# A graph network's first stage: the first two tiles share the weights, and the edge counts start with the third tile

## The chip, the cores and the metric

The kernel runs on one core of one Trainium2 chip. The metric is the device time of one execution in microseconds (us); lower is better. Engines are called as in the profile: PE (TensorE matmul), PEld (its weight load), DVE (VectorE), ACT (ScalarE), POOL (GpSimd), SP (SyncE, which issues most DMAs). PEq, DVEq, SPq and ACTq are the sequencers of these engines.

## What is computed

The input is x (1250 nodes, 1024 features) and 40,000 edges, sorted by their destination. The first block of the reference, cut to what matters:

```python
norm_x = weight * (x * rsqrt(mean(x**2) + EPS))
out = norm_x @ W_root + bias                    # 1024 -> 286
for r in range(2):
    w = (edge_type == r)
    sums = segment_sum(norm_x[src] @ W_rel[r] * w[:, None], dst)
    cnt = segment_sum(w, dst)
    out = out + sums / maximum(cnt, 1)[:, None]
x = layernorm(x + x + elu(out) @ wo)
```

A second block follows (an encoder, three rounds of summing neighbours with a small perceptron, a decoder). The change doesn't touch it.

## The kernel before, in words

The nodes are cut into T = 10 tiles of P = 125. Stage 1 does two things side by side.

**The projections.** For each tile, PE turns x (8 blocks of 128 features, `turn(q, v)` turns four of them into PSUM bank 6 + q), ACT copies them to `xnT` with the norm's weight as scale (`weigh(q)`), and PE multiplies each block by the 858 columns of the three weight matrices in `w_all` (`products(u, v)`, L781, two matrix products of 429 columns for block u). After block 7 ACT writes the tile out (`evacuate`: `y_root`, `y_hi`, `y_f`), and POOL makes `y_lo` from it (L388).

**The edge counts.** The edges stand in G = 80 rows of 500. For each row DVE builds one-hot codes in bf16: `codes` (L1234), `lows` (L1226) and `weighed_codes` (L1239). PE multiplies them (`count(b)`, L759, four small products), and DVE adds the two halves of the result into `cnt` (`place`, L1259) at a column that it reads from `mini` with `bases` (L1251). There are two sets of buffers, so the codes of row g + 2 are built while row g is placed. ACT takes finished columns of `cnt` apart into `adj`, a part of DONE columns at a time (`part(k, cols)`).

Everything is ordered by hand: each engine runs its own list, with semaphores between them. Tile 0 goes through the weights alone, in a list of its own. Its blocks wait for five pieces of the weights (`PIECES`: blocks 0, 1, 2 and 3, 4 and 5, 6 and 7), and between its blocks PE turns the edge data into PSUM (`turn_edges`, L752; the bounds of the rows, L836). From tile 1 on, PE does a row of edges before each block and one more at block 4: UG = 9 rows a tile, and the last tile has the 8 that are left. On PE and DVE tiles 1 to 8 run in a loop of two tiles; the last tile is written out behind it. For each tile, DVE also takes one reciprocal at the sixth row (L1270).

Stage 2 (`relations`, L937 and L939) multiplies `adj` by `y_hi` and `y_lo`. PE begins it when `adj_done` is set, which DVE does behind the last placed row (L1323), when the first part of `adj` is made, and when the `y_lo` of all tiles but the last is there. SP loads `cb_b` for it when `adj_done` is set and the last product of stage 1 is done (L304).

At the start SP issues x of tile 0, the norm's weight, the five pieces of the weights, and then x of tile 1. ACT's queue issues the three lists of the edges (`dst_i`, `src_i`, `typ_i`, L504).

Of the kernel before, what the change touches and what calls it, by code (L numbers as in the profile page):

```python
# [26 lines left out]
P = 125  # L27
# [24 lines left out]
DONE = 2 * P  # L52
FAR = 1e6
ROUND = 1.5 * 2 ** 18
UG = KD + 1
# [8 lines left out]
def graph_kernel(nc, x, src, dst, typ, ln_w, w_rel, w_root, conv_b, wo, g_in, b_in, w1, b1, w2, b2,  # L64
                 wa, ba, wb, bb, ng, nb, wd1, bd1, wd2, bd2, g_out, b_out, out):
    with ExitStack() as ctx:
# [28 lines left out]
        lo_base = y_base + size([P, T, YH], F32R)  # L95
        y_f = at(lo_base, "y_f", [P, T, 2 * F], F32)
# [144 lines left out]
        tails_set = sem("tails_set")  # L241
        second_set, parted, codes_set = sem("second_set"), sem("parted"), sem("codes_set")
# [38 lines left out]
        def _(sp):  # L281
# [151 lines left out]
        def _(act):  # L433
            for s in (xnT_copied, y_copied, hT_lo, r1_done, d1_done):
                act.sem_inc(s, 1)
# [31 lines left out]
            def evacuate(t, v):  # L467

                wait_apart(act, proj_mm, 1 + t * 2 + 2)
# [11 lines left out]
            def tile_of_1(t, v, uses, last, cleared=None, complete=None):  # L481
# [14 lines left out]
                if complete is not None:  # L496
                    act.wait_ge(counts_free, complete * (2 * UG) + 2 * UG + 2)
                    part(complete, bass.ds(complete * DONE, DONE))
# [4 lines left out]
            for a, d, done in ((dst_i, dst, dst_in), (src_i, src, src_in), (typ_i, typ, typ_in)):  # L503
                act.dma_start(a[:], d.rearrange("(g e) -> g e", g=G)).then_inc(done, 16)  # L504
# [3 lines left out]
            act.wait_ge(xnT_ps, 1)  # L508
            weigh(0)
            act.wait_ge(xnT_ps, 2)  # L510
            weigh(1)
            squares(0, 0)
            root_of(0, 0)
            act.wait_ge(edges_ps, 1)
            act.copy(value[:, 0:G], pb[0:P, 4, 160:160 + J * G].rearrange("p (j g) -> p g j", j=J)).then_inc(far_copied, 1)
            act.wait_ge(codes_ready, 1)
            act.copy(farC[:, 0:G], pb[0:P, 1, 0:J * G].rearrange("p (j g) -> p g j", j=J)).then_inc(far_copied, 1)
            act.wait_ge(xnT_ps, 3)
            act.wait_ge(proj_mm, 1 + 1)
            weigh(0)  # L520
            squares(1, 1)
            root_of(1, 1)
            evacuate(0, 0)
            tile_of_1(1, 1, 64, False, C0)
            tile_of_1(2, 0, 64, False)
            with act.Fori(1, T // 2 - 2) as i:
                tile_of_1(i * 2 + 1, 1, i * 32 + 64, False, i * CS + C0)
                tile_of_1(i * 2 + 2, 0, i * 32 + 64, False, None, i - 1)
            tile_of_1(T - 3, 1, 32 * (T // 2 - 1) + 32, False)
            tile_of_1(T - 2, 0, 32 * (T // 2 - 1) + 32, False, None, T // 2 - 3)  # L530
            tile_of_1(T - 1, 1, None, True, None, T // 2 - 2)
            act.wait_ge(counts_free, G + 2)
            part(T // 2 - 1, slice(N - DONE, N))
# [212 lines left out]
        def _(pe):  # L746
# [3 lines left out]
            def turn_edges(f, a, c0=0):  # L750
                for j in range(J):
                    ins = pe.transpose(pb[0:P, f, c0 + j * G:c0 + (j + 1) * G], a[:, j * P:(j + 1) * P], ident[0:G, 0:G])  # L752
# [33 lines left out]
            def tile_of_1(t, v, g0, odd, rows, uses):  # L786

                def row(r):
                    pe.wait_ge(onehots, g0 + r + 1)
                    pe.wait_ge(counts_free, g0 + r + 1)  # L790
                    count((odd + r) % 2).then_inc(counts_mm, 1)

                extra = rows - KD
                for u in range(KD):
                    row(u if u <= 4 else u + extra)
                    if u == 0:
                        pe.wait_ge(xnT_copied, 1 + t * 2)
                        turn(1, v)
                        pe.wait_ge(xnT_copied, 1 + t * 2 + 1)
                        pe.wait_ge(y_copied, t)  # L800
                    if u == 4:
# [4 lines left out]
                        if extra:  # L806
                            row(5)
# [16 lines left out]
            warm(2, 5)  # L824
            for u in range(KD):
                if u == 0:
                    pe.wait_ge(xnT_copied, 1 + 1)
                if u == 4:
                    pe.wait_ge(xnT_copied, 1 + 2)
                for q, ks in enumerate(PIECES):  # L830
                    if u == ks[0]:
                        pe.wait_ge(w_in[q], 48)
                if u == 2:
                    pe.wait_ge(bounds_ready, 1)
                    for i in range(2 * H):
                        ins = pe.transpose(pb[0:1, 4 + i // H, i % H * G:(i % H + 1) * G], bounds[:, i:i + 1], ident[0:G, 0:G])  # L836
                    ins.then_inc(bounds_ps, 1)
                if u == 4:
                    pe.wait_ge(lows_ready, 1)
                    turn_edges(0, e_low)  # L840
                if u == 5:
                    pe.wait_ge(edges_ready, 1)
                    pe.wait_ge(prep, 9)
                    turn_edges(4, e_val, 160)
                    turn_edges(1, e_code).then_inc(edges_ps, 1)
                if u == KD - 1:
                    pe.wait_ge(xs_in[1], 32)
                    turn(0, 1)
                products(u, 0)
# [789 lines left out]
```

## Time and profile before

| what | value |
|---|---|
| median of 3 runs | 577.02 us (575.8 to 577.03) |
| the profiled execution: its own time | 575.35 us |
| its span, first to last instruction | 573.5 us |
| PE / PEld busy | 556.0 us (97%) / 399.0 us (70%) |
| DVE / ACT / POOL busy | 371.2 us (65%) / 243.3 us (42%) / 101.6 us (18%) |
| the first product of stage 1 starts | 8.82 us |
| stage 2 starts | 158.05 us |

The span leaves out 1.85 us of the execution's own time. The matrix products' ends are modelled, so PE can look busy where it is waiting; starts are the safer figure. Consecutive instructions of DVE overlap by a few tens of nanoseconds, so for DVE, too, the distance from start to start is what is counted below.

### The profile page before, as it was taken

The numbers are of one execution on the slowest core, as the hardware profiler recorded it, in microseconds if no ns is written. First come the engines' busy times: TensorE is split into PE (matmuls) and PEld (weight loads), VectorE is DVE, ScalarE is ACT, GpSimd is POOL, SyncE is SP. The second block draws the span as 40 slices with busy tenths as digits, with TensorE's granted clock in tenths as the row PEclk, the third lists the DMA queues.
The fourth block names the chain that finished last, engine by engine and source line by source line (L and its number), as shares of the span: only waits on it lengthen the run. The fifth ranks groups of instructions, "written<-read, shape, count | busy, mean of one in ns | idle before, by whom it ended". The sixth has DMA issues, their size and how long they took to land.

```text
span 573.5 us, 8850 instructions
## 1 busy us (share of the span) xinstructions
PE 556.0 (97%) x2708; PEld 399.0 (70%) x2708; DVE 371.2 (65%) x1070; ACT 243.3 (42%) x484; POOL 101.6 (18%) x80
## 2 busy tenths in 40 slices
PE   7999999999999999999999999999999999999992
PEld 3555555555598989888889888868868867555541
DVE  8588888888748898987331130048658667855555
ACT  3553464636565555652222121023232233367555
POOL 4010000000000000030544442102202220132130
PEclk9999999999999999999999999999999999999997
DMA  8511000111031312147200001500100100022123
GB/s 263 159 38 36 24 25 24 36 36 36 2 93 38 73 37 72 37 136 210 101 2 0 0 0 40 191 1 1 38 0 0 37 0 2 0 73 68 39 73 107
DMA packets 20963, 30.77 MB, mean 54 GB/s; under 512 B 5458, under 2 KB 15404, under 8 KB 20928
## 3 DMA queue, kind: packets, MB, share of 16 engines
q1 hardware_dynamic: 20512, 29.66, 17.6%
q10 hardware_dynamic: 416, 0.67, 0.4%
q8 instruction: 19, 0.31, 0.2%
q14 instruction: 16, 0.13, 0.1%
HBM read 25.20 MB, written 5.12 MB: 53 GB/s over the span
## 4 chain that ended last, share of the span: by engine, by line
PE 77%; DVE 9%; DVEq 5%; issue 5%; DMA 2%; SPq 1%; ACT 1%; POOL 0%
PE banks L989 12%; PE banks L1075 12%; PE banks L906 12%; PE banks L781 7%; PE banks L874 5%; PE banks L1011 5%; PE banks L1001 4%; PE banks L937 4%; PE banks L939 4%; DVEq L1251 3%; PE banks L916 3%; PE banks L1065 3%; DVE cnt L1259 2%; DVE oh_both L1239 2%; DVE oh_both L1234 1%
## 5 line engine op out<-in xcount | busy, mean ns | idle before, releaser
L781 PE MATMUL banks<-w_all,xnT 128*125 128x429 f32 x320 | 131.8, 535 | 1.3 <-DMA w_all<-in_L_gnn_W_rel 1.3
L781 PEld LDWEIGHTS banks<-w_all,xnT 128*125 128x125 f32 x320 | 54.0, 188 | 30.4 <-issue 28.6
L906 PE MATMUL banks<-hT,w_s 128*128 128x250 f32 x320 | 68.9, 375 | 0.1
L906 PEld LDWEIGHTS banks<-hT,w_s 128*128 128x128 f32 x320 | 60.3, 190 | 8.4 <-issue 1.4
L937 PE MATMUL banks<-y_hi,adj 125*125 125x288 f32 x200 | 55.2, 304 | 0.5 <-issue 0.5
L1259 DVE TENSOR_TENSOR cnt<-cnt,banks 125x110 f32 x160 | 42.4, 265 | 18.1 <-issue 12.6
L939 PE MATMUL banks<-y_lo,adj 125*125 125x286 f32 x200 | 53.5, 295 | 0.0
L1406 DVE TENSOR_SCALAR hT<-banks,g_c,b_c 128x125 f32<-128x125 f32 x60 | 19.4, 399 | 45.1 <-PE banks L891 45.0
L989 PE MATMUL banks<-adj,h_hi 125*128 125x250 f32 (+1 forms) x180 | 48.3, 367 | 0.2
L759 PEld LDWEIGHTS banks<-oh_both,oh_low 125*128 125x128 bf16 x320 | 23.1, 98 | 34.9 <-issue 20.1
L989 PE MATMUL banks<-adj,h_lo 125*128 125x250 f32 (+1 forms) x180 | 45.7, 353 | 0.0
L1075 PE MATMUL banks<-wd_s,dT 128*125 128x512 f32 x96 | 42.7, 592 | 0.0
L399 POOL TENSOR_TENSOR h_lo<-h,h_hi 125x256 fp32r<-125x256 f32 x30 | 21.8, 733 | 108.5 <-ACT h_hi L608 108.5
L937 PEld LDWEIGHTS banks<-y_hi,adj 125*125 125x125 f32 x200 | 37.2, 186 | 3.8 <-issue 3.8
L388 POOL TENSOR_TENSOR y_lo<-y_f,y_hi 125x572 fp32r<-125x572 f32 x10 | 12.8, 1276 | 140.6 <-ACT y_f L479 140.6
L939 PEld LDWEIGHTS banks<-y_lo,adj 125*125 125x125 f32 x200 | 37.3, 187 | 0.0
L874 PE MATMUL banks<-wo_s,yT 128*125 128x256 f32 x160 | 36.2, 379 | 0.0
L463 ACT ACTIVATE xnT<-banks,lnw 128x125 f32<-128x125 f32 x80 | 22.7, 385 | 29.4 <-PE banks L775 29.4
L1226 DVE TENSOR_TENSOR oh_low<-iota_l,edge 125x512 bf16<-125x512 f16 x80 | 34.4, 430 | 0.1
L989 PEld LDWEIGHTS banks<-adj,h_hi 125*128 125x128 f32 x180 | 29.6, 189 | 6.0 <-issue 2.1
L1234 DVE TENSOR_TENSOR oh_both<-iota_m,edge 125x440 bf16<-125x440 f16 x80 | 33.4, 418 | 0.0
L989 PEld LDWEIGHTS banks<-adj,h_lo 125*128 125x128 f32 x180 | 30.1, 189 | 4.6
(222 smaller groups left out, 943.0 us busy)
## 6 DMA issues: line engine op xcount, KB each, us to landing
xt<-in_x SPq DMA_DIRECT2D x15, 448.0 KB
out_x<-ot SPq DMA_DIRECT2D x9, 448.0 KB
w_s<-in_L_gnn_W SPq DMA_DIRECT2D x5, 512.0 KB, 6.4
xn<-in_x SPq DMA_DIRECT2D x5, 448.0 KB
wd_s<-in_L_gnn_Wd SPq DMA_DIRECT2D x1, 2048.0 KB, 13.5
w_all<-in_L_gnn_W_rel SPq DMA_DIRECT2D x6, 286.0 KB, 6.7
wo_s<-in_L_gnn_wo_weight SPq DMA_DIRECT2D x1, 1024.0 KB, 6.1
w_all<-in_L_gnn_W_root SPq DMA_DIRECT2D x3, 286.0 KB, 6.3
```

The source lines that it names most:

```text
L759: ins = pe.matmul(pb[:, b, q * C:(q + 1) * C], oh_low[:, b, q, :, j], oh_both[:, b, q, :, j], start=(j == 0), stop=(j == JH - 1))
L781: ins = pe.matmul(pb[0:P, 2 + 2 * v + n, 0:FH], xnT[:, u], w_all[:, u, n * FH:(n + 1) * FH], start=(u == 0), stop=(u == KD - 1))
L874: pe.matmul(pb[0:P, 4 + q, 512 - QW:512], yT[:, i], wo_s[:, i, q * QW:(q + 1) * QW], start=(i == 0), stop=False)
L906: ins = pe.matmul(pb[:, b0 if f == 0 else 4 + f % 2, 0:2 * P], w1_s[:, k, f * 128:(f + 1) * 128], hT[:, k], start=(k == 0), stop=(k == KD ...
L937: pe.matmul(pb[0:P, b + r, 0:F + 2], mine, y_hi[:, s, r * (F + 2):(r + 1) * (F + 2)].bitcast(kind), start=(s == 0), stop=False)
L939: ins = pe.matmul(pb[0:P, b + r, w0:w0 + F], mine, y_lo[:, s, r * F:(r + 1) * F].bitcast(kind), start=False, stop=(s == T - 1))
L989: ins = pe.matmul(pb[:, 3 * f + c, 0:n], part[:, s, f * 128:(f + 1) * 128], adj[:, 0, s, c0:c0 + n], start=(s == 0 and part is h_hi), stop ...
L1011: ins = pe.matmul(pb[0:P, 6 + t % 2, 0:HB], rT[:, k, t * P:(t + 1) * P], wb_s[:, k], start=(k == 0), stop=(k == K2 - 1))
L1075: ins = pe.matmul(pb[0:P, 2 + 2 * u + q], (dT, dT_odd)[c % 2][:, k, u * P:(u + 1) * P], wd2_s[:, k, q * 512:(q + 1) * 512], start=(k == 0) ...
L1226: return dve.tensor_tensor(oh_low[:, b], both(iota_l, LOW), spread_out(edge[:, 0], g, LOW), ALU.is_equal)
L1234: return dve.tensor_tensor(oh_both[:, b], both(iota_m, C), spread_out(edge[:, 1], g, C), ALU.is_equal)
L1259: dve.tensor_tensor(cols, cols, window(b, q), ALU.add).then_inc(done, 1)
```

## The change

The first two tiles go through the weights together: blocks 0 and 1 of tile 0, blocks 0 and 1 of tile 1, blocks 2 and 3 of tile 0, and so on. Tile 1 gets a second buffer for its turned x (`xnT1`), and its own turns stand between its blocks and those of tile 0. The edge counts begin with tile 2, and all eight tiles from there on have UG = 10 rows, all of them in the loop. Columns of `adj` are made in parts of 300 (`PARTED`). SP issues x of tile 1 behind the second piece of the weights, and the edge lists, which ACT's queue issued before, behind the third.

```diff
-DONE = 2 * P
+DONE = 300
+PARTED = (0, DONE, 2 * DONE, 3 * DONE, 1060, N)
-UG = KD + 1
+UG = KD + 2
+        xnT1 = at(lo_base + 2 * 4 * 2 * F, "xnT1", [128, KD, P], F32)
...
             load_x(0, 0)
             sp.dma_start(lnw8[:], ln_w.rearrange("(k p) -> k p", p=128)).then_inc(lnw_in, 16)
-            for q in range(len(PIECES)):
-                load_w(sp, q)
+            load_w(sp, 0)
+            load_w(sp, 1)
             load_x(1, 1)
+            load_w(sp, 2)
+            for a, d, done in ((dst_i, dst, dst_in), (src_i, src, src_in), (typ_i, typ, typ_in)):
+                sp.dma_start(a[:], d.rearrange("(g e) -> g e", g=G)).then_inc(done, 16)
+            load_w(sp, 3)
+            load_w(sp, 4)
...
+            def weigh_blocks(t, turned):
+                for k in range(KD):
+                    act.wait_ge(xnT_ps, 1 + 2 * t + k // 4)
+                    act.activation(turned[:, k], pb[:, 6 + k // 4, k % 4 * P:(k % 4 + 1) * P], ACT.Copy,
+                                   scale=lnw[:, k:k + 1]).then_inc(first_turned, 1)
+            weigh_blocks(0, xnT)
             squares(0, 0)
             root_of(0, 0)
+            weigh_blocks(1, xnT1)
+            squares(1, 1)
+            root_of(1, 1)
+            act.wait_ge(xs_in[0], 64)
+            act.wait_ge(xn_rstd, 1)
+            squares(2, 0)
+            root_of(2, 0)
...
-            evacuate(0, 0)
-            tile_of_1(1, 1, 64, False, C0)
-            tile_of_1(2, 0, 64, False)
+            evacuate(0, 0, 4)
+            evacuate(1, 1, 5)
+            tile_of_1(2, 0, 64, False, C0)
+            tile_of_1(3, 1, 96, False)
...
                 for u in range(KD):
-                    row(u if u <= 4 else u + extra)
+                    row(u + (u > 0) + (u > 4))
                     if u == 0:
                         pe.wait_ge(xnT_copied, 1 + t * 2)
                         turn(1, v)
+                        row(1)
...
-            warm(2, 5)
-            for u in range(KD):
+            warm(1, 5)
+            def first_products(u, t):
+                pe.wait_ge(first_turned, KD * t + u + 1)
+                for n in range(2):
+                    ins = pe.matmul(pb[0:P, 2 + 2 * t + n, 0:FH], (xnT, xnT1)[t][:, u], w_all[:, u, n * FH:(n + 1) * FH],
+                                    start=(u == 0), stop=(u == KD - 1))
+            for u0 in range(0, KD, 2):
+                for t in range(2):
+                    if t == 1 and u0 == 0:
+                        pe.wait_ge(xs_in[1], 32)
+                        pe.wait_ge(first_turned, KD)
+                        turn(0, 1)
+                        turn(1, 1)
+                    if t == 1 and u0 == 2:
+                        pe.wait_ge(bounds_ready, 1)
...
+                    if t == 1 and u0 == 4:
+                        pe.wait_ge(lows_ready, 1)
+                        pe.wait_ge(edges_ready, 1)
...
+                        turn_edges(0, e_low)
+                        turn_edges(7, e_val)
+                        turn_edges(1, e_code).then_inc(edges_ps, 1)
+                    if t == 0 and u0 == 6:
+                        pe.wait_ge(xs_in[0], 64)
+                        turn(0, 0)
+                    for u in (u0, u0 + 1):
+                        for q, ks in enumerate(PIECES):
+                            if u == ks[0] and t == 0:
+                                pe.wait_ge(w_in[q], 48)
+                        first_products(u, t)
...
-            with pe.Fori(0, T // 2 - 1) as i:
-                tile_of_1(i * 2 + 1, 1, i * (2 * UG), 0, UG, i * 32 + 64)
-                tile_of_1(i * 2 + 2, 0, i * (2 * UG) + UG, UG % 2, UG, i * 32 + 64)
+            with pe.Fori(0, T // 2 - 2) as i:
+                tile_of_1(i * 2 + 2, 0, i * (2 * UG), i * 32 + 64)
+                tile_of_1(i * 2 + 3, 1, i * (2 * UG) + UG, i * 32 + 96)
...
-            tile_of_1(T - 1, 1, (T - 2) * UG, 0, G - (T - 2) * UG, None)
+            tile_of_1(T - 2, 0, 6 * UG, 32 * (T // 2))
+            tile_of_1(T - 1, 1, 7 * UG, None)
...
                 with dve.Fori(0, T // 2 - 1) as i:
                     dve.wait_ge(adj_rest, i + 1)
-                    tile_of_1(i * 2 + 1, 1, i * (2 * UG), 0, UG, placed)
-                    tile_of_1(i * 2 + 2, 0, i * (2 * UG) + UG, UG % 2, UG, placed)
-                tile_of_1(T - 1, 1, (T - 2) * UG, 0, G - (T - 2) * UG, placed)
+                    tile_of_1(i * 2 + 2, 0, i * (2 * UG), placed)
+                    tile_of_1(i * 2 + 3, 1, i * (2 * UG) + UG, placed)
```

DVE now builds codes for two rows beyond the last (before, it left them out: the lines `more` and `if more:` are gone), and its test of the data (`gaps`, `signs`, `bign`: which column each row may touch, and when) has the new bounds of 300, 600, 900 and 1060 columns in place of multiples of 250.

## Rows read from the trace of the kernel before

**Rows 1.** The page: busy time of each engine over the span.

```profile
PE 556.0 (97%) x2708; PEld 399.0 (70%) x2708; DVE 371.2 (65%) x1070; ACT 243.3 (42%) x484; POOL 101.6 (18%) x80
```

**Rows 2.** Busy time in two stretches, one tile each: PE, PEld, DVE, ACT, POOL, clock.

```profile
113.50:128.76 15.26, 15.05 (x80) 8.30 (x77) 13.22 (x47) 5.54 (x16) 1.23 (x1) 1.00 0.12 34
128.76:143.57 14.81, 14.81 (x81) 8.40 (x77) 13.18 (x48) 10.02 (x18) 1.34 (x1) 1.00 0.12 35
```

**Rows 3.** Who waited for whom, 20 to 158 us: in total, times, longest.

```profile
PEld banks L759 <- DVE oh_both L1239: 13.8, 44, 1.2
```

**Rows 4.** The chain that ended last: start, length, piece.

```profile
15.63 0.40 PE banks L752 x4
17.51 0.83 PE banks L752 x8
21.27 0.43 PE banks L775 x4
21.70 1.45 PE banks L781 x4
```

**Rows 5.** PE in order of time: start, length, instruction.

```profile
120.72 0.37 PE L759 MATMUL banks<-oh_both,oh_low 125*128 125x110 bf16 x4
120.94 0.60 PE L775 MATMUL banks<-ident,xt 125*128 125x125 f32 x4
121.70 0.39 PE L759 MATMUL banks<-oh_both,oh_low 125*128 125x110 bf16 x4 [0.17 <-DVE oh_both L1239]
...
123.43 0.37 PE L759 MATMUL banks<-oh_both,oh_low 125*128 125x110 bf16 x4
```

**Rows 6.** DVE in order of time: the first row of edges, and two in the loop.

```profile
23.77 0.38 DVE L1234 TENSOR_TENSOR oh_both<-iota_m,edge 125x440 bf16<-125x440 f16 x1
...
87.24 0.37 DVE L1234 TENSOR_TENSOR oh_both<-iota_m,edge 125x440 bf16<-125x440 f16 x1
...
88.80 0.38 DVE L1234 TENSOR_TENSOR oh_both<-iota_m,edge 125x440 bf16<-125x440 f16 x1
```

**Rows 7.** DVE in order of time: behind POOL, and around the loop's ends.

```profile
71.39 0.97 DVE L1234 TENSOR_TENSOR oh_both<-iota_m,edge 125x440 bf16<-125x440 f16 x1
...
83.00 0.38 DVE L1234 TENSOR_TENSOR oh_both<-iota_m,edge 125x440 bf16<-125x440 f16 x1
...
85.13 0.38 DVE L1234 TENSOR_TENSOR oh_both<-iota_m,edge 125x440 bf16<-125x440 f16 x1
...
115.22 0.38 DVE L1234 TENSOR_TENSOR oh_both<-iota_m,edge 125x440 bf16<-125x440 f16 x1
```

**Rows 8.** POOL in order of time.

```profile
70.91 1.20 POOL L388 TENSOR_TENSOR y_lo<-y_f,y_hi 125x572 fp32r<-125x572 f32 x1 [14.64 <-ACT y_f L479]
```

**Rows 9.** The lead-in, PE and DVE in order of time.

```profile
7.76 0.66 DVE L1161 TENSOR_REDUCE fourths<-dst_i 80x4 f32<-80x500 int32 x1
...
8.82 3.12 PE L781 MATMUL banks<-w_all,xnT 128*125 128x429 f32 x8 [1.26 <-DMA w_all<-in_L_gnn_W_rel]
...
12.22 0.86 DVE L1180 SCALAR_TENSOR_TENSOR e_code<-dst_i,bounds,e_blk 80x250 f32<-80x250 int32 x2
12.27 0.44 PE L836 MATMUL banks<-ident,bounds 80*1 80x80 f32 x4 [0.32 <-DMA w_all<-in_L_gnn_W_rel]
...
22.98 0.37 PE L759 MATMUL banks<-oh_both,oh_low 125*128 125x110 bf16 x4
```

**Rows 10.** DMA rate, 0 to 60 us in 40 slices of 1.5 us.

```profile
GB/s 0 221 161 258 317 304 349 355 353 366 390 303 268 46 5 0 52 284 5 0 11 0 0 0 0 5 101 240 5 0 0 0 0 0 0 5 145 197 0 0
```

**Rows 11.** The end of stage 1, PE in order of time.

```profile
158.05 0.37 PE L937 MATMUL banks<-y_hi,adj 125*125 125x288 f32 x1 [0.47 <-issue]
...
168.22 0.43 PE L866 MATMUL banks<-ident,ybuf 125*128 125x125 f32 x2 [0.40 <-DVE tails L1355]
```

**Rows 12.** Busy time in two stretches at the span's end; columns as in Rows 2.

```profile
563.00:567.00 4.00, 0.15 (x1) 0.00 (x0) 3.41 (x10) 2.72 (x5) 0.00 (x0) 1.00 0.01 3
567.00:571.00 4.00, 0.00 (x0) 0.00 (x0) 2.25 (x9) 2.61 (x6) 0.00 (x0) 0.50 0.44 138
```

More of the change, by code:

```diff
@@ L433, in _ @@
         def _(act):
-            for s in (xnT_copied, y_copied, hT_lo, r1_done, d1_done):
+            for s in (xnT_copied, xnT_copied, xnT_copied, xnT_copied, xnT_copied, y_copied, hT_lo, r1_done, d1_done):
                 act.sem_inc(s, 1)
@@ L496, in tile_of_1 @@
                 if complete is not None:
-                    act.wait_ge(counts_free, complete * (2 * UG) + 2 * UG + 2)
-                    part(complete, bass.ds(complete * DONE, DONE))
+                    k, cols, rows = complete
+                    act.wait_ge(counts_free, rows + 2)
+                    part(k, cols)
                 evacuate(t, v)
@@ L532, in _ @@
+            tile_of_1(T - 2, 0, 32 * (T // 2), False, None, (2, slice(PARTED[2], PARTED[3]), 6 * UG))
+            tile_of_1(T - 1, 1, None, True, None, (3, slice(PARTED[3], PARTED[4]), 7 * UG))
             act.wait_ge(counts_free, G + 2)
-            part(T // 2 - 1, slice(N - DONE, N))
+            part(4, slice(PARTED[4], N))
             def elu_parts_of(t):
@@ L784, in products, with tile_of_1 @@
                     ins.then_inc(proj_mm, 1)
-            def tile_of_1(t, v, g0, odd, rows, uses):
+            def tile_of_1(t, v, g0, uses):
                 def row(r):
@@ L805, in tile_of_1 @@
                             turn(0, 1 - v)
-                        if extra:
-                            row(5)
+                        row(6)
                     products(u, v)
@@ L823, in _ @@
             turn(1, 0)
-            warm(2, 5)
-            for u in range(KD):
[L826 to L849, printed above, removed]
+            warm(1, 5)
@@ new lines, in first_products @@
+            def first_products(u, t):
[3 more added lines that the diff above has]
+                                    start=(u == 0), stop=(u == KD - 1))
+                if u in (3, KD - 1):
+                    ins.then_inc(proj_mm, 1)
+            for u0 in range(0, KD, 2):
[7 more added lines that the diff above has]
+                        pe.wait_ge(bounds_ready, 1)
+                        for i in range(2 * H):
+                            ins = pe.transpose(pb[0:1, i // H, i % H * G:(i % H + 1) * G], bounds[:, i:i + 1], ident[0:G, 0:G])
+                        ins.then_inc(bounds_ps, 1)
+                    if t == 1 and u0 == 4:
+                        pe.wait_ge(lows_ready, 1)
+                        pe.wait_ge(edges_ready, 1)
+                        pe.wait_ge(prep, 9)
+                        pe.wait_ge(first_turned, 2 * KD)
+                        turn_edges(0, e_low)
[9 more added lines that the diff above has]
+                        first_products(u, t)
@@ L925, in relations @@
                         pe.wait_ge(pre_elu, t - 1)
-                    if t % 2 == 0:
-                        pe.wait_ge(parted, t // 2 + 1)
+                    pe.wait_ge(parted, sum(c0 < (t + 1) * P for c0 in PARTED[:-1]))
                     b = 2 * (t % 2)
@@ L1261, in place, with tile_of_1 @@
                     dve.sem_inc(done, 1)
-            def tile_of_1(t, v, g0, odd, rows, placed):
+            def tile_of_1(t, v, g0, placed):
                 base = bases(g0)
-                for u in range(rows):
+                for u in range(UG):
                     if u == 5:
@@ L1274, in tile_of_1 @@
                     place(base, b, 0, placed, first_added)
-                    more = rows == UG or u + 2 < rows
-                    if more:
-                        codes(g + 2, b).then_inc(codes_set, 1)
-                        lows(g + 2, b)
+                    codes(g + 2, b).then_inc(codes_set, 1)
+                    lows(g + 2, b)
                     dve.wait_ge(first_added, g + 1)
                     place(base, b, 1, placed, counts_free)
-                    if more:
-                        weighed_codes(g + 2, b).then_inc(onehots, 1)
-                    if u + 1 < rows:
+                    weighed_codes(g + 2, b).then_inc(onehots, 1)
+                    if u + 1 < UG:
                         base = bases(g + 1)
```

49 lines of the change are left out of this document (21 added, 28 removed).

## The prediction

> **What bounds the kernel now.** I read the page first, then the stretches of stage 1, then each engine's beat in it. By the page PE is busy 97% of the span and DVE 65% [rows 1], which reads like a kernel bound by PE alone. The stretches of stage 1 say nearly the same: in two tiles PE is busy 15.05 of 15.26 us and 14.81 of 14.81 us, DVE 13.22 and 13.18 [rows 2]. But the table of waits has PE's weight loads for the edge rows waiting 44 times for DVE's one-hot codes [rows 3]. So the question for this stage is how near DVE is to being the bound, and the starts of its instructions answer that better than busy time.
>
> *PE's beat.* The two products of one block take 1.45 us, four turns 0.43 us [rows 4]. The tile from 128.76 to 143.57 us took 14.81 us with no wait [rows 2]; it has eight blocks, nine edge rows and eight turns, so an edge row costs (14.81 - 8 x 1.45 - 2 x 0.43) / 9 = 0.26 us. From 121.70 to 123.43, one edge row and one block, it is 1.73 - 1.45 = 0.28. With four turns between two rows they are 0.98 us apart, with a wait for DVE in it, against 0.26 + 0.43 = 0.69 [rows 5]. The tile ahead of the undisturbed one took 15.26: it waited 0.45 us [rows 2].
>
> *DVE's beat.* Inside the loop one row of edges takes DVE 1.56 us from code to code (87.24 to 88.80), and this beat is the same in some 50 of the 70 rows [rows 6]. It is DVE's own speed: it is faster than PE's 1.45 + 0.26 = 1.71, so between the waits DVE is catching up. The other rows are longer. One per tile is long because its code takes 0.97 us where it takes 0.38 otherwise, while POOL makes `y_lo` [rows 7, 8]. At the loop's end the distance is 85.13 - 83.00 = 2.13, that is 0.57 more [rows 7]. All in all two tiles, 18 rows, took DVE 115.22 - 85.13 = 30.09 us [rows 7]. 18 x 1.56 is 28.08, so 2.01 us are extras of the pair: twice POOL (0.55 each), once the loop's end (0.57), and 0.34 for two reciprocals and small things. PE alone needs 2 x 14.81 = 29.62 for the same pair. DVE is thus already the bound of the loop, by 0.5 us a pair, and nothing is left for a tenth row.
>
> **The change, part by part.**
>
> *The start.* Before, PE waits until 8.82 us for the first piece of the weights, 1.26 us of it as the product's last wait [rows 9]. The piece is issued as before, but ACT's queue no longer puts 0.48 MB of edges beside it. At the 258 to 317 GB/s of those slices [rows 10] 0.48 MB are some 1.6 us. The first product could so come up to 1.3 us earlier (then x's turns, and what PE runs to keep warm, end at about 7.5) or no earlier. I take the middle, 8.0 us; ends 7.5 and 8.8.
>
> *The lead-in.* From there to the first edge row PE has 16 blocks, 16 x 1.45 = 23.2; twice four turns for tile 1 and four for tile 2, 1.29; the bounds, 0.44, and the edge data, 0.40 + 0.83 [rows 4]: 26.2 us. Behind tile 1's turns PE waits for ACT's first copy, some 0.2. Sum 26.4, so the first edge row is at 8.0 + 26.4 = 34.4 us, where it was at 22.98 [rows 9]. The difference, 11.4, is the second tile's 11.6 of products and 0.4 of turns, less what the start gives back.
>
> *What the shared weights save.* Before, the only later wait for the weights ended at 12.27 and was 0.3 us on PE [rows 9]. That goes away; there was hardly a DMA stall in tile 0 to remove. New waits: x of tile 1 is now wanted at 8.0 + 2.9 = 10.9. Ahead of it are x, two pieces of weights and itself, 1.9 MB, which at the rates of [rows 10] had moved by 9.0 us. Then it needs its turn and landing, so between 0 and 1 us of wait; I take 0. The edges come behind 2.8 MB, that is at about 13.3 us instead of 7.8. DVE's work on them, 12.22 + 0.86 - 7.76 = 5.3 us [rows 9], ends at about 18.6. PE wants the bounds at 8.0 + 10.2 = 18.2, which DVE makes about 2.3 us after the first list, at 15.6, and the rest at 24.3. The cover is thin by 2.6 us at the first place and wide at the second. The codes of rows 0 and 1 are made well ahead of 34.4. The later pieces of the weights land before 18 us [rows 10] and are wanted at 21 and 27. All this costs nothing. With the two ends of the start and of these waits the first edge row is at 33.9 to 36.2.
>
> *The edge rows.* They stay 80, with the same instructions on PE (L759) and DVE (L1234, L1226, L1239, L1259), but nothing of them is done before 34.4. PE's tile of ten rows is 14.81 + 0.26 = 15.07. DVE's pair of tiles is 20 rows, 20 x 1.56 + 2.01 = 33.2 us, or 16.6 a tile: 1.5 more than PE's. So DVE sets the beat, and PE, with only two sets of codes between them, waits for it at nearly every row; it is those waits that take the place of the gain. DVE begins its first code 23.77 - 22.98 = 0.8 us after PE's first row [rows 6, 9], at 35.2. Four pairs less the last loop's end are 4 x 33.2 - 0.6 = 132.2, so DVE is done at 167.4. Ends: if POOL no longer held DVE up at all, 4 x 1.1 less; if each pair had 0.2 more, 0.8 more. I take the pair as measured, since POOL's `y_lo` follows each tile's evacuation just as now. The tile that stood behind the loop, where rows are written out, is now in the loop as well; that is in the 33.2. So are the codes of two rows beyond the last, which before were left out.
>
> *The end of the stage.* Before, PE's own products ended the stage: stage 2 starts at 158.05 [rows 11]. Now `adj_done` does, at 167.4, as DVE is about one row behind PE: PE's last product is over at about 166.3, so ACT's evacuation and POOL's last `y_lo` are early rather than late. Smaller parts of `adj` (300, 160 and 190 columns) are off the path, since stage 2 wants the first at once, when it has long been made, and the last for its ninth tile. `cb_b` is loaded when `adj_done` is set. It was issued 0.39 us ahead of stage 2 and the chain through it made PE wait 0.40 at 168.22 [rows 11]; now it is issued at the same moment, so 0 to 0.4 more. I take 0.2.
>
> **The sum.** Stage 2 at 167.4 instead of 158.05 is +9.35, `cb_b` +0.2: +9.5 us, and everything behind shifts by it. Against the profiled execution, 575.35 + 9.5 = 584.9. The median of the runs is 1.67 above that execution, so the forecast is 577.0 + 9.5 = 586.5 us.
>
> **Rivals.**
> *PE stays the bound and the change gains* (faster). For this speaks busy time: PE 15.05 against DVE 13.22 in one tile [rows 2]. Then eight tiles of 15.07 from 34.4 end at 155.0, and stage 2 starts at 155.4, 2.6 us earlier: 574.4 us. It decides if DVE does ten rows with all extras in under 15.07, 1.51 a row instead of 1.66. Against it: the row of 1.56 repeats unchanged over the loop. The Trainium skill ("Perfetto Trace Analysis", Identifying the Most-Contended Engine) takes occupancy as the fair measure for Vector, and by it DVE at 13.2 of 15 has room for one more row; the starts in this trace say that it hasn't, as a fixed 0.2 us per row is spent between instructions.
> *Half and half* (about the same). If DVE had slack that I don't see, as rows that wait for PE without the profile saying so, a row might be 1.45 and the end of the stage near 158: 577 us. The pair of 30.09 against PE's 29.62 speaks against it.
> *TensorE's clock falls* (much slower). PE will now wait for a good 1 us in each 16. If it fell from 2.4 to 1.2 GHz, a block would take 2.9 us, a tile some 27, and each tile at the low clock cost 10 us more. In this trace the granted clock stays 1.00 with such waits as there are [rows 2], and falls to 0.50 only after PE has had nothing to do for some 4 us at the end [rows 12]. The Trainium skill ("TensorE: Matmul & The Clock Gate", HAM oscillation) tells of gaps that throttle PE again and again, there while PE waits for whole transfers; no run so far shows it here, where the longest single wait is 1.2 [rows 3].
> *The test of the data fails.* Row 20 must start at column 300 or later; evenly spread edges put it at 1250 x 20 / 80 = 312. If it failed, all counts would be made again by the slow way, 114 sweeps over 80 rows, at over 1 us a row more than 9 ms. The reference's edges are spread closely enough.
>
> **Chances.** DVE-bound as summed: 0.86; its own range is 584.5 to 588.5, from the first row's place (-0.5 to +1.8), the pairs (most of -4.4 is excluded by the rows, I keep -1.5) and the 0.6 us by which runs differ. PE-bound gain: 0.05. Half and half, anywhere from 575 to 583: 0.04. Slower than 589, by a late transfer or the clock: 0.04. The test: 0.01. For 8 in 10 the range is 583.3 to 589.0. Faster by over 0.3% (what a measurement can tell, 1.7 us) 0.06, within it 0.02, slower 0.92.
>
> **What would show it.** The first product at about 8 us and the first edge row (L759) at 34 to 35. L1234 every 1.56 us and every 33.2 us per pair, to the end. The waits of L759 for L1239 up from 13.8 us to some 25 to 30 (80 rows, 1.5 us in each tile on top of now). PE's busy share in 36 to 166 us below its share now, its clock 1.00. Stage 2 at about 167.4, released by DVE's memset (L1323), and the distance from there to the end as before. The forecast is wrong if DVE's row gets shorter than 1.51 with extras, if the first row comes much later than 36, or if stage 2 and what follows change length.

## The result, and the profile after

The changed kernel takes 587.71 us (median of 4 runs, 586.64 to 588.37), the kernel before 577.02 beside it: a ratio of 1.0191, 95% interval 1.0171 to 1.0210. The forecast was 586.5 us, in a range from 583.3 to 589.0. By the medians the change costs 10.7 us, where the sum had 9.5. The profiled execution took 586.64 us with a span of 584.8, that is 11.3 us more than the one before; the traces below explain this difference of 11.3.

The page of the changed kernel, busy time of each engine; then two of its stretches, as in [rows 2], the first in the loop of the counted tiles, the second the end of the stage:

```profile
PE 558.8 (96%) x2707; PEld 398.3 (68%) x2707; DVE 373.4 (64%) x1077; ACT 243.7 (42%) x484; POOL 101.7 (17%) x80
```

```profile
96.00:126.00 30.00, 28.11 (x144) 15.25 (x142) 26.36 (x91) 16.70 (x31) 2.51 (x2) 1.00 0.12 34
...
156.00:168.00 12.00, 10.79 (x52) 5.69 (x52) 10.60 (x40) 1.64 (x2) 0.00 (x0) 1.00 0.01 1
```

PE is at 94% and 90% there, where a tile before had 99 to 100% [rows 2]. The granted clock is 1.00 there, as in all of stage 1. The engine that now sets the pace shows 26.36 of 30 us busy, 88%: DVE doesn't look full by its busy time either.

Who waited for whom, 34 to 168 us of the changed kernel, against [rows 3]:

```profile
PEld banks L776 <- DVE oh_both L1271: 32.2, 68, 2.0
...
PE banks L776 <- DVE oh_both L1271: 9.4, 16, 1.3
```

L776 is the edge row's product on PE (L759 before), L1271 the weighed codes (L1239 before). For the 80 rows there are 68 waits of the weight loads for DVE, against 44, and they add up to 32.2 us, a little above the 25 to 30 forecast.

PE in order of time: the first product, tile 1's turns, the bounds, the first edge row and the first product of stage 2, against [rows 9, 11]:

```profile
7.48 3.15 PE L846 MATMUL banks<-w_all,xnT 128*125 128x429 f32 x8
...
11.01 1.08 PE L792 MATMUL banks<-ident,xn 125*128 125x125 f32 x8 [0.39 <-DMA xn<-in_x]
...
18.00 0.44 PE L861 MATMUL banks<-ident,bounds 80*1 80x80 f32 x4
...
34.49 0.37 PE L776 MATMUL banks<-oh_both,oh_low 125*128 125x110 bf16 x4
...
169.46 0.37 PE L966 MATMUL banks<-y_hi,adj 125*125 125x288 f32 x1 [1.65 <-DVE small L1351]
```

The first product is 1.3 us earlier than before and the first edge row 11.5 later. Stage 2 is 11.4 later, and it waits for DVE's memset (L1351), as the forecast had it; before, it waited for no other engine. From there to the end of the span it is 415.3 us, before 415.45: nothing behind stage 1 changed.

DVE in order of time, the code of edge rows 0, 20, 40, 60 and 79 (L1266 is L1234 before), two rows next to each other, the `lows` of row 20 (L1258, L1226 before), and the memset, against [rows 6, 7]:

```profile
35.27 0.38 DVE L1266 TENSOR_TENSOR oh_both<-iota_m,edge 125x440 bf16<-125x440 f16 x1
...
69.44 0.38 DVE L1266 TENSOR_TENSOR oh_both<-iota_m,edge 125x440 bf16<-125x440 f16 x1
69.74 1.42 DVE L1258 TENSOR_TENSOR oh_low<-iota_l,edge 125x512 bf16<-125x512 f16 x1
...
91.30 0.38 DVE L1266 TENSOR_TENSOR oh_both<-iota_m,edge 125x440 bf16<-125x440 f16 x1
...
92.86 0.38 DVE L1266 TENSOR_TENSOR oh_both<-iota_m,edge 125x440 bf16<-125x440 f16 x1
...
102.97 0.38 DVE L1266 TENSOR_TENSOR oh_both<-iota_m,edge 125x440 bf16<-125x440 f16 x1
...
136.29 0.38 DVE L1266 TENSOR_TENSOR oh_both<-iota_m,edge 125x440 bf16<-125x440 f16 x1
...
167.50 0.38 DVE L1266 TENSOR_TENSOR oh_both<-iota_m,edge 125x440 bf16<-125x440 f16 x1
168.64 0.06 DVE L1351 MEMSET small<- 125x1 f32 x1
```

The beat (the distance from one code to the next) is 92.86 - 91.30 = 1.56 us, as before. From the starts of rows 0, 20, 40 and 60, the first three pairs of tiles take 34.17, 33.53 and 33.32 us; the sum had 33.2 for each.

### The profile page after: what moved, and what is told of

It reads as the page before. It is cut to its first block, busy times and chain, and to the rows that moved or that the text cites. A ratio compares the mean times of both kernels' runs of the same rounds, so it can differ in the third digit from the quotient of the medians.

```text
span 584.8 us, 8886 instructions
## 1 busy us (share of the span) xinstructions
PE 558.8 (96%) x2707; PEld 398.3 (68%) x2707; DVE 373.4 (64%) x1077; ACT 243.7 (42%) x484; POOL 101.7 (17%) x80
## 4 chain that ended last, share of the span: by engine, by line
PE 70%; DVE 12%; DVEq 7%; issue 6%; DMA 2%; ACT 1%; SPq 1%
PE banks L1018 12%; PE banks L1104 12%; PE banks L936 10%; PE banks L904 5%; PE banks L966 5%; DVEq L1283 5%; PE banks L968 5%; PE banks L1040 4%; PE banks L1030 4%; DVE cnt L1291 4%; PE banks L846 4%; PE banks L946 3%; PE banks L1094 3%; DVE oh_both L1271 2%; DVE oh_low L1258 2%
## 5 line engine op out<-in xcount | busy, mean ns | idle before, releaser
L798 PE MATMUL banks<-w_all,xnT 128*125 128x429 f32 x256 | 106.4, 537 | 0.0
L798 PEld LDWEIGHTS banks<-w_all,xnT 128*125 128x125 f32 x256 | 42.9, 188 | 22.1 <-issue 22.1
L1291 DVE TENSOR_TENSOR cnt<-cnt,banks 125x110 f32 x160 | 42.5, 266 | 20.6 <-issue 11.4
L776 PEld LDWEIGHTS banks<-oh_both,oh_low 125*128 125x128 bf16 x320 | 21.5, 98 | 43.9 <-DVE oh_both L1271 32.2
L776 PE MATMUL banks<-oh_both,oh_low 125*128 125x110 bf16 x320 | 29.9, 215 | 9.7 <-DVE oh_both L1271 9.4
L1258 DVE TENSOR_TENSOR oh_low<-iota_l,edge 125x512 bf16<-125x512 f16 x82 | 36.3, 443 | 0.0
L1271 DVE TENSOR_TENSOR oh_both<-oh_both,value 125x440 bf16<-125x440 bf16 x82 | 33.7, 411 | 0.0
L472 ACT ACTIVATE xnT<-banks,lnw 128x125 f32<-128x125 f32 x64 | 18.3, 386 | 36.2 <-PE banks L792 36.2
```

The costliest lines, as they stand in the source:

```text
L776: ins = pe.matmul(pb[:, b, q * C:(q + 1) * C], oh_low[:, b, q, :, j], oh_both[:, b, q, :, j], start=(j == 0), stop=(j == JH - 1))
L798: ins = pe.matmul(pb[0:P, 2 + 2 * v + n, 0:FH], xnT[:, u], w_all[:, u, n * FH:(n + 1) * FH], start=(u == 0), stop=(u == KD - 1))
L1258: return dve.tensor_tensor(oh_low[:, b], both(iota_l, LOW), spread_out(edge[:, 0], g, LOW), ALU.is_equal)
L1271: return dve.tensor_tensor(oh_both[:, b], oh_both[:, b], spread_out(value, g, C), ALU.mult)
L1291: dve.tensor_tensor(cols, cols, window(b, q), ALU.add).then_inc(done, 1)
```

## The experiments

Two theories stood at first. A: DVE's beat bounds the counted tiles. B: the cost lies in PE's list or in the lead-in, and DVE's waits are a symptom. Ratios are to the kernel before, run beside each on the same chip, with 95% intervals. Names with a_ are versions of the changed kernel, with b_ of the kernel before.

### The loop written out: a_unrolled, b_unrolled

```diff
+                if placed:
+                    for i in range(T // 2 - 1):
+                        dve.wait_ge(adj_rest, i + 1)
+                        tile_of_1(i * 2 + 2, 0, i * (2 * UG), placed)
+                        tile_of_1(i * 2 + 3, 1, i * (2 * UG) + UG, placed)
+                    return
                 with dve.Fori(0, T // 2 - 1) as i:
```

In b_unrolled the same is done with the loop of the kernel before.

> The changed kernel with DVE's loop over the counted tiles written out, so that columns and waits of every edge row are constants (same instructions otherwise, nothing else touched). Theory A (DVE's beat of 1.56 us a row plus extras bounds the counted tiles, and 0.2 us of each row is register work of the loop): rows fall to the 1.36 us of the written-out tile of the kernel before, a pair of tiles to 20 x 1.36 + 1.5 = 28.7 us, below PE's 30.1, so PE becomes the bound, the first edge row stays at 34.5 us, stage 2 starts at 34.5 + 8 x 15.07 + 0.5 = about 155.6 instead of 169.5 us, and the time falls by 13 to 14 us, to about 574 us, under the kernel before. Theory B (the cost comes with PE's list or with the lead-in: a tenth row a tile, more turns and waits between the first blocks, and DVE's waits are only a symptom): stage 2 moves by less than 3 us and the time stays above 584 us.

> The kernel before with the same edit, DVE's loop written out. Theory A: the loop was bound by DVE by only 0.5 us a pair, so at most the waits of 1.6 us in all are won and the time falls by 1 to 2 us, to about 575.5 us. Theory B has no reason for a difference: within 0.5 us.

a_unrolled took 574.07 us, ratio 0.9964 (0.9949 to 0.9979); b_unrolled 573.34, ratio 0.9957 (0.9943 to 0.9972). The same edit takes 13.6 us off the changed kernel (587.71; by the two ratios, each to the kernel before beside it, 13.1) and 2.7 off the kernel before (575.99 beside it), where 1 to 2 were expected. B falls: PE's list and the lead-in are untouched in both, and the cost is gone. DVE and then PE of a_unrolled, in order of time:

```profile
89.78 0.38 DVE L1266 TENSOR_TENSOR oh_both<-iota_m,edge 125x440 bf16<-125x440 f16 x1
...
91.14 0.38 DVE L1266 TENSOR_TENSOR oh_both<-iota_m,edge 125x440 bf16<-125x440 f16 x1
```

```profile
34.87 0.37 PE L776 MATMUL banks<-oh_both,oh_low 125*128 125x110 bf16 x4
...
157.19 0.37 PE L966 MATMUL banks<-y_hi,adj 125*125 125x288 f32 x1 [1.21 <-issue]
```

A DVE row takes 91.14 - 89.78 = 1.36 us, as expected. Stage 2 begins at 157.19, 1.6 us after the 155.6 expected: the first row was 0.4 us later, the eight tiles took 0.5 more, and 1.2 us pass between PE's last product and stage 2, where the sum had 0.5.

What the loop costs is not the load of the columns. The sequencer's instructions on the line that loads them, first in the changed kernel, then in a_unrolled (nanoseconds: least, median, most):

```profile
L1283 DVEq TENSOR_LOAD <-mini x79: 523/528/545, 35.9 to 166.6; - x79
L1283 DVEq FUSED_REGOPS  x78: 71/71/75, 37.4 to 166.5; - x78
```

```profile
L1283 DVEq TENSOR_LOAD <-mini x79: 520/526/534, 36.0 to 153.6; - x79
```

The loads stay as they are. A register operation of 0.07 us a row is gone with the loop; how the rest of the 0.20 us divides isn't shown.

In b_unrolled stage 2 begins at 155.55, 1.6 us before that of a_unrolled. So with DVE out of the way the shared weights win nothing: 574.07 against 573.34 us, with intervals that overlap. Where their earlier start went can be read in the two traces, PE in order of time, first a_unrolled, then b_unrolled:

```profile
6.97 1.65 PE L846 MATMUL banks<-w_all,xnT 128*125 128x429 f32 x4
9.62 1.71 PE L846 MATMUL banks<-w_all,xnT 128*125 128x429 f32 x4 [1.00 <-DMA w_all<-in_L_gnn_W_rel]
```

```profile
8.70 3.12 PE L781 MATMUL banks<-w_all,xnT 128*125 128x429 f32 x8 [1.47 <-ACT xnT L463]
...
155.55 0.37 PE L937 MATMUL banks<-y_hi,adj 125*125 125x288 f32 x1 [0.72 <-issue]
```

The first product comes 1.7 us earlier, but PE then waits 1.00 us for the second piece of the weights, and at the end of the stage it loses 0.5 more than b_unrolled (1.21 against 0.72). The rest lies between these two places and wasn't taken apart.

### Less data work: a_short, b_short

```diff
-                return dve.tensor_tensor(oh_both[:, b], oh_both[:, b], spread_out(value, g, C), ALU.mult)
+                return dve.tensor_tensor(oh_both[:, b, :, 0:1], oh_both[:, b, :, 0:1], spread_out(value, g, 1), ALU.mult)
```

> The changed kernel in which DVE weighs one column of the one-hot codes in place of all 55 (so the edges' types are left out of the counts, and the output isn't the reference's). Loop and instruction count stay. Theory A: a DVE row gets about 0.2 us shorter (0.30 us from start to start for that instruction now, about 0.1 with one column), 1.36 a row, 20 x 1.36 + 2.0 = 29.2 us a pair against PE's 30.1, stage 2 at about 156 us, time 573 to 575 us. Theory B: within 3 us of 587.

> The kernel before with the same edit (types left out of the counts). Theory A: 1 to 2 us less than the kernel before, as PE is the bound as soon as DVE has any slack. Theory B: within 0.5 us of the kernel before.

a_short took 586.78 us, ratio 1.0184 (1.0164 to 1.0203): within 1 us of the changed kernel, a miss of theory A's 573 to 575. b_short took 574.44, 0.9967 (0.9952 to 0.9982), 1.5 us less than the kernel before. DVE of a_short in order of time:

```profile
90.50 0.38 DVE L1266 TENSOR_TENSOR oh_both<-iota_m,edge 125x440 bf16<-125x440 f16 x1
...
91.31 0.16 DVE L1271 TENSOR_TENSOR oh_both<-oh_both,value 125x4 bf16<-125x4 bf16 x1
91.87 0.27 DVE L1291 TENSOR_TENSOR cnt<-cnt,banks 125x110 f32 x1 [0.41 <-DVE cnt L1291]
```

The weighed codes take 0.16 us in place of 0.38, and the idle time behind them is 0.41 in place of 0.18. The beat stays 1.56 us (the codes before these came at 88.94). Shortening this instruction doesn't shorten it. The profile has another candidate, the sequencer: in each row it loads two columns from `mini` into registers (L1283, L1251 before), and does register work for the addresses and waits. The chain of a_short has the sequencer and idle time in each row where the data work was:

```profile
91.13 0.26 DVE cnt L1291
91.39 0.07 DVEq L1283
91.47 0.24 issue
...
91.87 0.10 DVE cnt L1291
```

b_short gained about what theory A had expected, but not for its reason: its beat is 1.56 us too. What became shorter are two rows in each pair, those beside POOL's operation. `weighed_codes` of such a row in the kernel before, and in b_short:

```profile
85.94 1.20 DVE L1239 TENSOR_TENSOR oh_both<-oh_both,value 125x440 bf16<-125x440 bf16 x1
```

```profile
86.42 0.98 DVE L1239 TENSOR_TENSOR oh_both<-oh_both,value 125x4 bf16<-125x4 bf16 x1
```

Such rows take 1.9 us in place of 2.1. From the first code behind edge row 0 to the last it is 127.7 us in place of 129.2, that is 1.5 less.

### The load moved forward: a_early, b_early, a_short_early

```diff
                     lows(g + 2, b)
+                    following = bases(g + 1) if u + 1 < UG else None
                     dve.wait_ge(first_added, g + 1)
                     place(base, b, 1, placed, counts_free)
                     weighed_codes(g + 2, b).then_inc(onehots, 1)
-                    if u + 1 < UG:
-                        base = bases(g + 1)
+                    base = following
```

> The changed kernel, loop kept, with one move in DVE's list: the load of the next row's two columns stands ahead of the second placement in place of behind the weighed codes. Theory A2 (the beat of 1.56 us is DVE's sequencer: the load of 0.53 us and the register work behind the second placement take 0.74 us, under which the weighed codes' 0.30 us lies for nothing): the load falls under the lows, the row takes 1.30 to 1.40 us, PE becomes the bound, and the time is that of the written-out loop, 573 to 575.5 us. Theory R (what the loop costs is register work for addresses and waits as such, wherever it stands): the row stays at 1.5 us or more and the time above 583 us.

> The kernel before with the same move. Theory A2: the same time as its written-out loop, 573 to 574.5 us (0.4% under the kernel before). Theory R: within 0.7 us of the kernel before.

> One look at the changed kernel with both the early load and the weighing of one column in place of 55 (the types are left out of the counts). Theory S: neither data work nor order matters while the sequencer has 1.54 us a row, so L1266 comes every 1.52 to 1.56 us and the time is 584 to 587 us. If the data work had become the bound once the load was moved, the row falls to 1.3 us and the time to 575.

a_early took 585.99 us, 1.0168 (1.0154 to 1.0183); b_early 575.09, 0.9988 (0.9977 to 1.0). Theory A2 falls: the load lies elsewhere, and the row still takes 1.53 to 1.56 us. DVE's code in a_early, and the sequencer's pieces of the chain between:

```profile
91.05 0.38 DVE L1266 TENSOR_TENSOR oh_both<-iota_m,edge 125x440 bf16<-125x440 f16 x1
...
92.58 0.38 DVE L1266 TENSOR_TENSOR oh_both<-iota_m,edge 125x440 bf16<-125x440 f16 x1
```

```profile
91.23 0.53 DVEq L1283
...
91.81 0.05 DVEq L1291
...
92.01 0.04 DVEq L1271
...
92.28 0.05 DVEq L1291
...
92.39 0.07 DVEq L1266
```

a_short_early, with both edits, took 582.94 us in its one execution. Two of its codes:

```profile
89.90 0.38 DVE L1266 TENSOR_TENSOR oh_both<-iota_m,edge 125x440 bf16<-125x440 f16 x1
...
91.43 0.38 DVE L1266 TENSOR_TENSOR oh_both<-iota_m,edge 125x440 bf16<-125x440 f16 x1
```

The rows take 1.53 to 1.54 us, as theory S expected. The time lies below its 584 to 587, and again it is the rows beside POOL that are shorter: seven of them by 1.9 us together against a_early. Neither the order nor 0.22 us less to compute made the common row shorter than about 1.5. Theory R, as it was put, had it right here, in that the order doesn't matter. Theory S brings the two together: the sequencer's own work per row, loads, register work and dispatches, adds up to some 1.54 us. That sum is an assumption. In the 1.54 us of the chain between the two codes of a_early, 0.74 are the sequencer's pieces shown above, 0.33 "issue" (time in which DVE waits for nothing that the profile shows) and 0.47 pieces of DVE's own instructions.

### Fewer loads: a_pairload, b_pairload, b_pair_even

```diff
+            def bases_of_two(g):
+                return nc.values_load_multi_w_load_instructions(
+                    mini[0:1, bass.ds(g * H, 2 * H)], engines=[mybir.EngineType.DVE], min_val=0, max_val=N,
...
-                base = bases(g0)
+                base = bases_of_two(g0)
...
-                    if u + 1 < UG:
-                        base = bases(g + 1)
+                    base = base[H:]
+                    if not base and u + 1 < UG:
+                        base = bases_of_two(g + 1)
```

> The changed kernel, loop kept, order kept, but the columns of two edge rows are loaded into registers at once, so one load in two goes away. Theory S (DVE's sequencer is the bound: per row it has some 1.54 us of loads, register work and dispatches in all, whatever their order, and 1.35 us of data work beside it): the row falls by half a load, 0.26 us, to what the data work takes, 1.35, PE becomes the bound, time 573 to 576 us. Theory R in its narrow form (the load is hidden, and only the register work for addresses and waits counts): the row stays above 1.5 us, time above 584 us.

> The kernel before with the same edit. Theory S: the time of its written-out loop, 573 to 574.5 us. Theory R: within 0.7 us of the kernel before.

a_pairload took 574.18 us, 0.9954 (0.9940 to 0.9969), with its stage 2 at 157.01: the loop is there, the instructions of DVE's data path are the same, and half of the loads is gone. Its codes in order of time:

```profile
85.05 0.38 DVE L1266 TENSOR_TENSOR oh_both<-iota_m,edge 125x440 bf16<-125x440 f16 x1
...
86.33 0.38 DVE L1266 TENSOR_TENSOR oh_both<-iota_m,edge 125x440 bf16<-125x440 f16 x1
...
87.70 0.38 DVE L1266 TENSOR_TENSOR oh_both<-iota_m,edge 125x440 bf16<-125x440 f16 x1
```

The rows take 1.29 and 1.37 us in turn. This is the test that theory S passes and both narrower forms fail: less work for the sequencer shortens the row, where less data work and another order did not. The loads got shorter as well as fewer, 0.34 us for two rows in place of 0.53 for each, so it isn't a clean halving.

b_pairload did not gain: 577.67 us, 1.0016 (1.0003 to 1.0028), 1.4 us above the kernel before, which is in neither theory's range. Not all of that need come from the loads: in its profiled execution the first edge row comes at 24.37 in place of 22.98, before any load counts, as the first products of the weights stand 0.7 us apart where they stand 0.4 apart otherwise. Its loads, first in tiles that begin at an even row, then in one that begins at an odd row (nanoseconds: least, median, most):

```profile
L1257 DVEq TENSOR_LOAD <-mini x5: 343/347/376, 23.9 to 37.0; - x5
```

```profile
L1257 DVEq TENSOR_LOAD <-mini x4: 960/968/972, 39.1 to 49.8; - x4
```

With nine rows a tile every second tile begins at an odd row, and its loads of four values start at 8 bytes past a multiple of 16. b_pair_even always loads from an even row; its edit against b_pairload, cut:

```diff
-            def tile_of_1(t, v, g0, odd, rows, placed):
-                base = bases_of_two(g0)
+            def tile_of_1(t, v, g0, odd, rows, placed, base=None):
+                base = base or bases_of_two(g0)
...
+                return base
...
-                    tile_of_1(i * 2 + 1, 1, i * (2 * UG), 0, UG, placed)
-                    tile_of_1(i * 2 + 2, 0, i * (2 * UG) + UG, UG % 2, UG, placed)
+                    left = tile_of_1(i * 2 + 1, 1, i * (2 * UG), 0, UG, placed)
+                    tile_of_1(i * 2 + 2, 0, i * (2 * UG) + UG, UG % 2, UG, placed, left)
```

> The kernel before with the columns of two edge rows loaded at once, as in its first such version, but always from an even row: the first tile of a pair hands its leftover columns to the second. In the first version the load of four values takes 0.34 us from even rows and 0.97 us from odd ones, and DVE's rows there are 1.29 and 2.00 us in turn. If the odd start is the cause (and theory S holds), every load takes 0.34 us, the rows average 1.35 us, PE becomes the bound in both tiles, and the time is that of the written-out loop, 573 to 574.5 us. If it is the second tile as such (its loads, its place in the loop), its loads stay near 0.97 us and the time at 576 to 578 us.

It took 574.14 us, 0.9962 (0.9945 to 0.9979), and all its 39 loads are short:

```profile
L1257 DVEq TENSOR_LOAD <-mini x39: 339/343/350, 26.3 to 150.5; - x39
```

### The start: a_actq, b_unrolled_sp

a_actq undoes the move of the edge lists from ACT's queue to SP's (the diff below). b_unrolled_sp makes that move in the kernel before with DVE's loop written out, behind the first piece of the weights.

```diff
-            for a, d, done in ((dst_i, dst, dst_in), (src_i, src, src_in), (typ_i, typ, typ_in)):
-                sp.dma_start(a[:], d.rearrange("(g e) -> g e", g=G)).then_inc(done, 16)
...
+            for a, d, done in ((dst_i, dst, dst_in), (src_i, src, src_in), (typ_i, typ, typ_in)):
+                act.dma_start(a[:], d.rearrange("(g e) -> g e", g=G)).then_inc(done, 16)
```

> The changed kernel with the edge lists issued from ACT's queue at the start, as in the kernel before (that part of the change undone). If DVE's beat from the first edge row on sets the time, only the start moves: the first piece of the weights lands later by up to 1.3 us, so first edge row at 34.5 to 35.8, time 586 to 588.5 us, and nothing is won by edges that are ready 7 us earlier. If the late edge lists were what costs (DVE's codes late, or PE waiting for the bounds), the time falls by 2 us or more.

> The kernel before with DVE's loop written out and the edge lists issued by SP behind the first piece of the weights instead of by ACT's queue. With PE the bound from the first product on, what the shared weights could win is the earlier start alone: the first product at 7.5 in place of 8.7 us, the edge lists landing at 9 to 10 us, DVE's work on them done by 15.5, so that PE waits for the bounds (wanted at 10.4, there at 11.5 to 12.5) by 1 to 2 us. Net between -1 and +1 us of the written-out loop's 573.3. A gain of 1 us would say that the start is worth having alone.

a_actq took 589.53 us, 1.0235 (1.0220 to 1.0251), 1 us above the most expected for it. Its first product and first edge row, PE in order of time:

```profile
8.63 4.84 PE L846 MATMUL banks<-w_all,xnT 128*125 128x429 f32 x8 [1.98 <-DMA w_all<-in_L_gnn_W_rel]
...
36.73 0.37 PE L776 MATMUL banks<-oh_both,oh_low 125*128 125x110 bf16 x4
```

The first product is 1.15 us later than in the changed kernel, and its eight matmul records stretch over 4.84 us in place of 3.15. The granted clock is low there. A stretch ahead of the first product and one behind it, columns as in [rows 2] (the clock is the third figure from the right):

```profile
6.66:8.60 1.94, 0.00 (x0) 0.00 (x0) 1.91 (x5) 1.94 (x8) 0.99 (x1) 1.00 1.09 292
...
9.60:12.00 2.40, 2.40 (x5) 1.05 (x4) 2.23 (x7) 0.07 (x1) 0.00 (x0) 0.50 1.03 234
```

PE did nothing for 1.98 us. Behind that the granted clock was 0.50 (1.2 of 2.4 GHz) from about 9.2 to 12.4 us, with PE at work all the time, and then 1.00 again. A product took 0.90 us there, where it takes 0.53 on average in the changed kernel's lead-in. In b_pairload's trace the first products are as slow at a recorded clock of 1.00, so that the clock alone makes them slow isn't shown, nor whether the other executions of a_actq had this. In the profiled one the first edge row comes 2.2 us later, and stage 2 too (171.66); the median is 1.8 us higher (2.5 by the ratios). Edge lists that are ready 7 us earlier win nothing, so the late lists weren't the cost.

b_unrolled_sp took 574.22, 0.9969 (0.9958 to 0.9980), within the expected range and no better than b_unrolled. The first product came 0.6 us earlier, but the wait behind it was not the expected one for the bounds. These were made at 10.0 us; PE came to them late, as it waited for a piece of the weights, which the edge lists were now issued ahead of:

```profile
12.72 0.44 PE L837 MATMUL banks<-ident,bounds 80*1 80x80 f32 x4 [1.23 <-DMA w_all<-in_L_gnn_W_rel]
```

## Why the prediction was right, point by point

**What bounds the kernel.** The prediction took DVE as the bound of the counted tiles, by 0.5 us a pair, and the tenth row as more than it can do. That is shown: with DVE's rows shortened from 1.56 to 1.35 us, in two ways that leave PE's list alone, the time falls by 13.6 and 13.5 us, more than the whole cost of the change (a_unrolled, a_pairload). The like edits give the kernel before only 1.7 to 2.7 us (b_pair_even, b_unrolled).

**The rule of busy time.** The rival that PE stays the bound is the time of a kernel whose DVE does a row in under 1.51 us: 574.4 us was worked out for it, and a_unrolled and a_pairload took 574.07 and 574.18. As it stands the kernel isn't that one. The Trainium skill ("Perfetto Trace Analysis", Identifying the Most-Contended Engine) takes occupancy, the share of time spent in instructions, to find the bottleneck, and for Vector as a fair measure. This case's trace does not agree: 88% of DVE's time looked busy while it set the pace and PE showed 94%. Work of the sequencer is not in these shares.

**The lead-in.** First product 7.48 (forecast 8.0, bounds 7.5 to 8.8), first edge row 34.49 (34.4). Here two errors cancel, which is luck: PE took 27.0 us from the one to the other where the sum had 26.4, as it waited for x of tile 1, for the weights and for ACT, some 1 us together, which I had at 0.2. The five other traces with this lead-in have the first edge row anywhere from 33.99 to 35.48. The new turns were miscounted in words: eight are new in the lead-in, 0.9 us, and not 0.4; the sum of 26.4 has them right. The bounds were ready when PE came to them at 18.00, as forecast, but only by 0.6 us, where I had worked with 2.6 of cover: the first edge list was reduced 1.8 us later than forecast.

**The edge rows.** DVE needed 167.50 - 35.27 = 132.2 us to the last row's code, where the sum had 132.2 - 1.56 = 130.6. This is the term that was too small, by 1.6 us, and the mechanism behind it was right. The first pair took 34.17, where two boundaries between rows had 0.3 us more each with no release seen. At the head of the second, `lows` took 1.42 us beside POOL, and the row 2.30 where the third pair has 2.12. The trace before had most of this. Its first three pairs begin at 23.77 [rows 6], at

```profile
54.84 0.38 DVE L1234 TENSOR_TENSOR oh_both<-iota_m,edge 125x440 bf16<-125x440 f16 x1
```

and at 85.13, and the third ends at 115.22 [rows 7]: 31.07, 30.29 and 30.09 us. I had taken the third, the calmest, for all four. The first two alone would have added 1.2 of the 1.6 us.

**The end of the stage.** DVE's memset releases stage 2, as said. From the last code to stage 2 it is 1.96 us, where the sum had 1.56: 0.4 more. Behind it, `cb_b` cost nothing that can be seen (0.2 forecast): SP issued it at 168.75, 0.71 us ahead of stage 2, and not at the same moment. The terms: 0.1 + 1.6 + 0.4, less 0.3 for `cb_b` and what follows, are 1.8 us, the difference between 11.3 and 9.5.

**What was missing.** The prediction called 1.56 us "DVE's own speed" and noted 0.2 us between instructions, but not whose they are. That left the number right and would have led a repair wrong: a_short took 0.22 us of data work out of each row and won nothing that can be told from no change. What the runs show is that taking work from the sequencer shortens the row. How the 1.56 us divide between loads, addresses, waits, dispatches and data work stays open. The other two rivals, the clock and the data's test, did not come up in the changed kernel: the clock is 1.00 in all of stage 1, and the rows are placed as before. The clock was nearer than the prediction had it, though. From the trace before it took some 4 us without work as what came ahead of a fall; in a_actq the clock fell after 1.98.

**The gain.** The change was to keep PE fed while the weights land. There was 0.3 us of such waiting behind the first product. Of the earlier start of 1.3 us, the waits of the lead-in took about half back: some 1.0 us, where the kernel before had 0.3. The rest can't be seen in the time, as DVE sets the pace from there. With DVE relieved in both kernels, their times can't be told apart.

## What to carry to other kernels

Before work of one engine is moved under the work of another, put its beat from start to start beside the other's time for the new share; busy shares of 88% and 94% didn't tell which of the two had room. If a beat doesn't shorten when the computing does, look at the sequencer. In this kernel half as many loads into registers, each twice as wide, or a written-out loop made DVE's row 0.2 us shorter, and 0.2 us less to compute did not. The best versions here are the kernel before with DVE's loop written out (573.34 us) or with its loads paired from even rows (574.14); the shared weights add nothing to them.

## What the runs showed of the hardware that was not expected

A load of two 4-byte values from a row in SBUF into DVE's registers took 0.53 us, a load of four 0.34 when it began at a multiple of 16 bytes, and 0.97 when it began 8 bytes past one. The wider load was thus cheaper than the narrow one, and where it begins was worth a factor of 2.8. All loads of two took 0.52 to 0.56 us, at even and odd rows alike.

In the profiled execution of a_actq the granted clock of TensorE went from 1.00 to 0.50 behind a stretch of 1.98 us without work. A stretch of 1.65 us at the same place in b_pair_even was followed by 1.00.
